# Scales by transposes and on-chip copies, K and V as single products between the transposes

## What is computed

```python
q = w8a8_linear(layernorm(x), wq, bq)          # rows and weights rounded to 127 levels
k, v = ctx @ wk.T + bk, ctx @ wv.T + bv        # fp32, 16 heads of 32
attn = softmax(q @ k.T / sqrt(32) + mask)
x = x + w8a8_linear(attn @ v, wo, bo)
h = gelu(int8_linear(layernorm(x), W1, B1))    # 512 -> 2048, scales per row
out = x + int8_linear(h, W2, B2)               # 2048 -> 512
```

## Time and profile before

| | |
|---|---|
| median of 3 runs | 748.97 us (744.27 to 751.18) |
| the profiled execution | 753.85 us, its span 751.9 us |
| granted TensorE clock, mean | 0.941 |
| instructions | 14564 |

### The profile page before, as it was taken

How to read it: one execution, slowest core, us unless ns; L and a number is a source line. 1 busy time by engine, 2 the same in 40 slices (tenths; PEclk the granted TensorE clock), 3 DMA queues, 4 the chain that set the end, 5 groups by cost and what they waited for, 6 DMA issues and landing times.

```text
span 751.9 us, 14564 instructions
## 1 busy us (share of the span) xinstructions
PE 633.2 (84%) x4936; PEld 474.4 (63%) x4986; DVE 469.8 (62%) x1101; ACT 444.6 (59%) x1085; POOL 300.4 (40%) x555
## 2 busy tenths in 40 slices
PE   1838779979797799989699899989897999998763
PEld 1736566857665576767668677867675686766421
DVE  6635667856774295667376665468554576856763
ACT  2316555757763384949369566668584587878400
POOL 4232433453544353545452444353461333231231
PEclk9988898998998899999899999999999999999967
DMA  9985297752324425451722525324323112201321
GB/s 290 254 87 129 69 173 182 231 90 67 59 51 79 45 40 100 34 95 39 68 72 38 99 17 111 52 49 39 98 52 67 35 36 54 55 24 13 64 49 42
DMA packets 92664, 61.07 MB, mean 81 GB/s; under 512 B 69952, under 2 KB 79936, under 8 KB 91952
## 3 DMA queue, kind: packets, MB, share of 16 engines
q1 hardware_dynamic: 92592, 60.15, 41.2%
HBM read 42.09 MB, written 3.69 MB: 61 GB/s over the span
## 4 chain that ended last, share of the span: by engine, by line
PE 43%; DMA 21%; DVE 11%; SPq 9%; issue 8%; POOL 5%; ACT 1%; DVEq 0%; POOLq 0%
PE ps_ring L869 10%; PE ps_t L889 7%; PE ps_ring L855 7%; DMA oqT<-o_q 5%; PE ps_ring L933 5%; DMA q_dram<-cols 4%; PE ps_s L880 4%; PE ps_ring L945 4%; PE ps_t L902 4%; SPq L344 3%; DMA hT<-h_q 3%; DMA yqT<-y_q 2%; DMA xT<-x_q 2%; DMA q_dram<-so_col 1%; DMA b_row<-in_w2T 1%
## 5 line engine op out<-in xcount | busy, mean ns | idle before, releaser
L577 ACT ACTIVATE probs<-probs,neg_max 112x375 f32<-112x375 f32 x256 | 153.6, 602 | 36.5 <-DVE neg_max L702 36.0
L587 ACT ACTIVATE pT<-ps_t 125x336 f32<-125x336 f32 x256 | 109.0, 446 | 93.3 <-PE ps_t L889 91.6
L702 DVE CUSTOM_DVE_ANT_0 probs<-ps_s,mask_in 112x375 f32<-112x375 f32 x256 | 127.0, 543 | 56.4 <-PE ps_s L880 49.0
L889 PE MATMUL ps_t<-ident,probs 112*125 112x112 f32 x768 | 149.5, 287 | 4.4 <-ACT probs L577 2.1
L889 PEld LDWEIGHTS ps_t<-ident,probs 112*125 112x125 f32 x768 | 125.3, 199 | 36.9 <-issue 17.2
L855 PE MATMUL ps_ring<-ctx_hi,wk_hi 128*128 128x376 f32 x256 | 95.6, 373 | 29.0 <-DVE wk_lo L608 15.8
L869 PE MATMUL ps_ring<-wv_hi,ctx_hi 128*125 128x512 f32 x192 | 86.3, 449 | 2.1 <-issue 2.0
L855 PE MATMUL ps_ring<-ctx_lo,wk_hi 128*128 128x376 f32 x256 | 87.8, 343 | 0.0
L855 PE MATMUL ps_ring<-ctx_hi,wk_lo 128*128 128x376 f32 x256 | 87.6, 342 | 0.0
L463 POOL TENSOR_TENSOR ctx_lo<-ctx_in,ctx_hi 128x376 fp32r<-128x376 f32 x64 | 66.7, 1068 | 49.7 <-ACT ctx_hi L557 48.8
L945 PE MATMUL ps_ring<-w_q,hT 128*128 128x512 bf16 x207 | 65.9, 417 | 19.0 <-DMA hT<-h_q 18.2
(11 more groups left out here) (107 smaller groups left out, 1071.4 us busy)
## 6 DMA issues: line engine op xcount, KB each, us to landing
ctx_in<-in_ctxT SPq DMA_DIRECT2D x32, 375.0 KB, 6.3
h<-in_w2T SPq DMA_DIRECT2D x4, 1024.0 KB, 9.0
b_row<-in_w2T SPq DMA_DIRECT2D x4, 1024.0 KB, 9.8
xres<-in_x SPq DMA_DIRECT2D x14, 256.0 KB, 2.8
x_in<-in_x SPq DMA_DIRECT2D x16, 224.0 KB, 4.3
out<-y SPq DMA_DIRECT2D x14, 256.0 KB, 2.7
mask_in<-in_mask SPq DMA_DIRECT2D x16, 164.1 KB, 3.9
w_q<-in_w1T SPq DMA_DIRECT2D x2, 1024.0 KB, 13.9
```

Source lines behind the costliest of these rows:

```text
L577: nc.scalar.activation(probs[:, hd % SP_RING, :], probs[:, hd % SP_RING, :], ACT.Exp, scale=-1.0, bias=neg_max[:, b % 2, hd:hd + 1], accum ...
L587: nc.scalar.activation(pT[0:LR, hd % PT_RING, :], att_bank("T", b, hd, 0)[0:LR, 0:LC * N], ACT.Copy).then_inc(pT_s, 1)
L702: nc.vector.tensor_tensor_reduce(out=probs[:, hd % SP_RING, :], in0=ps_s[hd % HG][0:N, 0:L], in1=mask_in[:, b % 2, :], scale=-1.0, scalar= ...
L889: last = nc.tensor.transpose(att_bank("T", b, hd, 0)[0:LR, lc * N:(lc + 1) * N], probs[:, hd % SP_RING, lc * LR:(lc + 1) * LR], ident[0:N, ...
```

## The change

x's scale: TensorE transposes the column, repeated over 128 columns, against the identity (`x`), which gives the repeated row in a `ps_t` bank; ScalarE copies it to `xs_bc`. `so` likewise (`O`), in a `ps_ring` bank. o's scale: one DMA from `o_s` to `os_col`, both in SBUF, per batch, two where the batch lies in two tiles (`p`, now `os_move`), with four columns instead of two. `s`, `l`, `e`, `f`, `i` are gone from the SP list. A letter `k` or `v` is now one product instead of three. All five lists are new. Counts of all other letters are the same.

```diff
-    "k": ("k", each(B, KC, KC)), "v": ("v", each(B, LC, KC)), "q": ("q", each(B)), "S": ("S", each(B, KC)),
+    "O": ("so", each()), "x": ("x_row", each(B)),
+    "k": ("k", each(B, KC, 3 * KC)), "v": ("v", each(B, LC, 3 * KC)), "q": ("q", each(B)), "S": ("S", each(B, KC)),
...
 PE_ORDER = (
-    "kkkkkkkkkkkkkkkkvvvvvvvvvvvvkkkkkkkkkkqkkkkkkvSvvvTTTvTTTTTTSTTTvMPvTTTTTTSTTTvTTTTTTPqTTTvTTTvTTTSvPvTTTTTTTTTk"
...
-    "TTTTSkdTdTdTdTdTdTddkPTkdTdTdTdTdTdkdTdTTTTTooookPkkkkkkkqSvvvvTTTTTTSuuuuuuTuTuTTTTuuuuTTTPuuuvvvTTTuvSTTTvvvvk"
...
-    "dTdTdTddPTdTdTTTTTTTPguuuuuuuuuuuuuuuuoooodddddddddddddddduuuuuuuuuuuuuuuudddddddddddddddd"
+    "xkkkvvvkkkvvkkkvvvkkkvvvvkkkkkkkkkkkkkkkkkkkkOkkkkvvvvvvvvvvvvvvvvvvvvvvvvkkkkkkqkkkkkkkkkkkkSkkkvvvvvvTTTTSTTTT"
...
+    "dSTkTkTkTkTTkqTkTkTkTkTTkkkTSoooovTvTvvvvvvvvvvvvPTvTvTvTvTvTvTvTvTvTvTvTvvvvvvuuuuvvvSvvPTuuuuuuuuTTuuuuTkTkTkk"
+    "kkkkkkSkTkTkTkTkTkTkkkkkkkkPTkTkTkTkTkTkkTkTkTkxSkkPgddddddddddddddddkTTkTkTkTTkkqTTkTkTkTTkkkTSoooovTvTvvvvvvvv"
...
+    "dddddPTTTddddooooddddTTTTTTTTTTTTTTTPPguuuuuuuuuuuuuuuuoooouuuuuuuuuuuuuuuudddddddddddddddddddddddddddddddd"
 )
 DVE_ORDER = (
...
-    "ySmSQqSSSSuSSSuSugSoSuSShhHymSQSSSudSSuSSquhSSSSuSSSSghoHSSSSySSSmQdguuouuhhHymQduuuuhhHd"
+    "SgodSSqSymQSSSSuSSuuSuShhSHSSgSoSSdSSymQSSSSSSuSuuuShghSHSSSoSSSSydmQgouuuuyhmhQHuuuuhhdHd"
 )
...
 POOL_ORDER = (
-    "nllllXrllllnqllllXnqllllXnqXllllnqbyrXllllHbynrqXHlllnlbyqrXnHllllXbynqrXnHllllbyqrXnHllllqXbynrHllllqXbynrHllll"
+    "nrXlllllllqnllXlllqnllllXnqXllqnllXbyqnrHlXlllnbyqrXHnlllqXlbyrHnllqXlbyrlHnllqXlbyrlHnllqXlbyrlHnllqXlbyrlHnllq"
...
 SP_ORDER = (
-    "rxmQCCWWWW1cmQWWWW1sCC1txXelCCft1slCCxXms2l2CpoCxX222s2lmxX2C2CpoisBlrYmxXCCpoiHrHYmslxXSHpHoiCrSsCYlxXmHsHpoCiC"
+    "WWWWcWxWWWrCCQm1Qm11xXCCtCt1CxXCCm222CC2po2xX2m22xXBCpoCmxXrYHpHoxXCSCmrYxXHHpoSCmxXrCYHHpoSCmxXrYCHHpoSCmxXrYCH"
...
+def parts(b):
+    cut = (b * N // P + 1) * P
+    return [(b * N, cut), (cut, (b + 1) * N)] if cut < (b + 1) * N else [(b * N, (b + 1) * N)]
...
+            def os_move(b):
+
                 sp.wait_ge(o_sc_s, b + 1)
-                sp.dma_start(os_dram[b * N:(b + 1) * N].unsqueeze(1), o_s[:]).then_inc(os_stored, 16)
-
-            def os_load(t):
-                sp.wait_ge(os_stored, 16 * batches_of(t))
-                wait_for(sp, y_mul, t - 1)
-                sp.dma_start(os_col[:, t % 2:t % 2 + 1], os_dram[t * P:(t + 1) * P].unsqueeze(1)).then_inc(os_in[t % 2], 16)
+                for row, end in parts(b):
+                    t = row // P
+                    wait_for(sp, y_mul, t - OS + 1)
+                    sp.dma_start(os_col[row % P:row % P + end - row, t % OS:t % OS + 1],
+                                 o_s[row - b * N:end - b * N, :]).then_inc(os_in, 16)
...
+            def x_row(b):
+                act.wait_ge(xrow_pe, b + 1)
+                wait_for(act, q_mul, b)
+                nc.scalar.activation(xs_bc[:], att_bank("x_row", b)[:, 0:N], ACT.Copy).then_inc(xs_s, 1)
...
+            def x_row(b):
+                pe.wait_ge(x_scaled, b + 1)
...
+                bank = att_free("x_row", b)
+                nc.tensor.transpose(bank[:, 0:N], x_s[:].broadcast_to([N, P]), ident[0:N, 0:N]).then_inc(xrow_pe, 1)
```

More of the change, by code:

```diff
@@ L37 @@
 ATT = 2
+OS = 4
 def each(*counts):
@@ L75 @@
     "1": ("w1_load", each(4)), "2": ("w2_load", each(8)), "B": ("b1_load", each()),
-    "e": ("so_store", each()), "f": ("so_load", each()),
-    "X": ("x_T", each(B)), "s": ("xs_store", each(B)), "l": ("xs_load", each(B)),
-    "o": ("o_T", each(B)), "p": ("os_store", each(B)), "i": ("os_load", each(TILES)),
+    "X": ("x_T", each(B)), "o": ("o_T", each(B)), "p": ("os_move", each(B)),
     "Y": ("y_T", each(TILES)), "H": ("h_T", each(TILES, 2)),
@@ L850, in k_unit @@
                 bank = bank_of("k", b, g, 0)
[L851 to L857 removed]
+                if part == 0:
+                    if b == 0:
+                        pe.wait_ge(w_lo_s, k + 1)
+                    pe.wait_ge(ctx_lo_s, KC * b + k + 1)
@@ L858, in k_unit, with v_unit @@
+                w_half, x_part = ((wk_hi, ctx_hi), (wk_hi, ctx_lo), (wk_lo, ctx_hi))[part]
+                last = nc.tensor.matmul(bank[:, 0:LP], w_half[:, k, cols], x_part[:, p, k, :],
+                                        start=(step == 0), stop=(step == 3 * KC - 1))
+                if step == 3 * KC - 1:
                     last.then_inc(k_pe, 1)
-            def v_unit(b, lc, k):
-                p, rows = b % 2, slice(lc * LR, (lc + 1) * LR)
-                if k == 0:
+            def v_unit(b, lc, step):
+                p, rows, k, part = b % 2, slice(lc * LR, (lc + 1) * LR), step // 3, step % 3
+                if step == 0:
@@ L863, in v_unit @@
                     ring_bank("v", b, lc, 0)
                 bank = bank_of("v", b, lc, 0)
-                if b == 0:
-                    pe.wait_ge(w_lo_s, KC + k + 1)
-                pe.wait_ge(ctx_lo_s, KC * b + k + 1)
-                for t, (x_part, w_half) in enumerate(((ctx_hi, wv_hi), (ctx_hi, wv_lo), (ctx_lo, wv_hi))):
-                    last = nc.tensor.matmul(bank[0:LR, :], x_part[:, p, k, rows], w_half[:, k, :],
-                                            start=(k == 0 and t == 0), stop=(k == KC - 1 and t == 2))
@@ L871, in v_unit @@
-                if k == KC - 1:
+                if part == 0:
+                    if b == 0:
+                        pe.wait_ge(w_lo_s, KC + k + 1)
+                    pe.wait_ge(ctx_lo_s, KC * b + k + 1)
+                x_part, w_half = ((ctx_hi, wv_hi), (ctx_hi, wv_lo), (ctx_lo, wv_hi))[part]
+                last = nc.tensor.matmul(bank[0:LR, :], x_part[:, p, k, rows], w_half[:, k, :],
+                                        start=(step == 0), stop=(step == 3 * KC - 1))
+                if step == 3 * KC - 1:
```

154 lines of the change are left out of this document (74 added, 80 removed).

## The result

The changed kernel takes 675.68 us (median of 4, 674.34 to 676.3), the kernel before 750.08 beside it (744.27 to 752.14): ratio 0.902, 95% interval 0.896 to 0.907. A few executions of a kernel come out slower for no reason of the kernel's own; they are left out of the medians and ranges in this text.

A forecast was written before the change was run, and what follows sets the result against it. TensorE's own work was taken to bound the middle, latency chains both ends. Terms of -20, -14, +7, -3, -11, +5, -4 sum to -40 us: 753.85 to 714 profiled, median 709, own range 698 to 722, wider range 682 to 742.

The forecast's parts named there:

- first rival: Idle time of the middle closes almost wholly, as the new pattern covers each chain: median 672 us; chance 0.17.
- What bounds the kernel: TensorE's own work bounds the middle, latency chains both ends; o's transpose (6.2 us) completes just after the store (7.3).
- Output scales, -20: On-chip copies land in 2.5 us instead of 7.3, nearly ending TensorE's wait before output projection: -20 us (-5 to -28.6).
- The other chains and the clock, -14: Waits before `up` and `down` and low clock behind idle stretches shrink in the new order: -14 us (0 to -40).
- K and V mixed, +7: Single products between transposes: 451 more lone transposes cost 4.5 us, 17 new ones 3: +7 us (+3 to +12).
- x's scales, -3: 32 transfers leave SP's queue for TensorE transposes and ScalarE copies; fewer table loads, cover not path: -3 us (0 to -10).
- The start, -11: K starts near 23 us, q near 40, scores near 45, first gather at 80 instead of 96: -11 us (0 to -20).
- The new slack, +5: Scores may wait for VectorE's mask, standing 1.3 us behind the transpose that frees the buffer: +5 us (0 to +36).
- rival "slower": Turn of transpose, mask and scores costs 2.5 us at each of 36 close places: 794 us; chance 0.12.
- The end, -4: Chains of y and o shorten at the end, against two absmax in y's chain (2.4 us): -4 us (0 to -8).
- The floor, 671: TensorE's busy 633 us plus the idle start and end (23 + 15) cannot go: 671 us.
- The signs it named: If right: oqT lands in 2.4-3 us, copies <3, oqT wait <8, first-last gather <590, scores <50, K >20.

The follow-up runs named there:

- path_only: The changed kernel's scale path (transposes on TensorE, on-chip copies) with the old order of the work; 679.64 us, ratio 0.917 to the kernel before.
- before_all_spread: Kernel before, only addresses changed: output scales 1,792 bytes apart in memory, x's scales 8 bytes apart; 674.68 us, ratio 0.912.
- dummy_store: Changed kernel plus one unread store per batch of 112 scales to neighbouring memory addresses, ahead of o's transposing DMA; 747.2 us.
- dummy_behind: Changed kernel plus one unread store per batch of 112 scales to neighbouring memory addresses, behind o's transposing DMA; 716.75 us.
- triples: Changed kernel with the three probability transposes of a head issued together where the first stood; 678.02 us.
- xs_memory: Changed kernel with x's scales alone stored to memory and loaded back, output scales still copied on chip; 745.16 us.
- start_tail: Changed kernel with start reordered (x's and context's loads first) and tile 13's norm no longer split by two row maxima; 667.77 us.
- before_spread: Kernel before with output scales stored 1,792 bytes apart in memory, x's scales as they were; 694.65 us, ratio 0.937.

## Why the prediction was wrong

Its first rival (the idle time closes almost wholly, 672 us) came true in its number, at a chance of 0.17, but not for its reason: it had the new pattern cover each chain, and path_only and before_all_spread reach 680 and 675 us with the old one. By its own steps:

**What bounds the kernel.** Right in kind. The link that it drew, "the transpose completes just after the store ahead of it", is shown by dummy_store. That only the transpose was held is the step that failed: the 6.3 us landing of the context's load stood on the same page of the profile, and in dummy_behind the context's load (6.8 us), x's load (7.9) and y's rows (8.8) behind the store are late as well. Nor was it memory as a target that made the store slow, as the prediction read the 7.3 us: to far addresses in memory it lands in 1.7, as the copies on chip do.

**Output scales, -20.** The copy landed in 1.7 us (taken: 2.5), the wait went wholly. In the middle it had been 26.4 us of the 34.9. The size of the wait was read rightly. The pattern with 16 d, 12 k, 13 T, a q and an S before `oooo` stands seven times in the list, not nine (and once with a second S), which changes nothing here. The remedy was not the copy on chip as such but any destination that isn't near.

**The other chains and the clock, -14.** The term most mis-sized. Of the middle's 53 us, 46 are idle time, 26 of them oqT's; so 20 are other waits (yqT 9.5, xT 5.2, hT some 5), and the clock rose from 0.96 to 1.00, at most 22 us more (half of 44). That makes 68; TensorE's other busy time must then have risen by some 15 in this stretch, of which the next term and the shifted K and V work (6) are a part. So this term gave up to 42 us (20 + 22), or 27 after all that grew (53 - 26), where the forecast took 14 within bounds of 0 and -40. The low clock was in the bound and hardly in the choice, although it follows the same waits that the first term had just removed. That these waits and the slow stretches came from the near stores, and not from an order that covered its chains unevenly, is shown by before_all_spread: the old order, middle 521 us, clock 1.00.

**K and V mixed, +7.** A lone transpose behaves as foreseen; TensorE in order of time:

```profile
156.90 0.26 PE L910 MATMUL ps_t<-ident,probs 112*125 112x112 f32 x1
156.93 0.42 PE L875 MATMUL ps_ring<-ctx_hi,wk_lo 128*128 128x376 f32 x1
157.19 0.26 PE L910 MATMUL ps_t<-ident,probs 112*125 112x112 f32 x1
```

0.29 per pair, so 0.12 for the transpose. The 4.5 us for 451 more of them don't show against triples (612.2 and 612.0 us busy). Of the +7, the rest was for new transposes, which are 20 and not 17, as `O` is four.

**x's scales, -3.** The table loads fell to 26 as counted. But x's stores were costed as cover, and xs_memory puts stores and loads together at 69 us in the new order. The trace of before had two signs of it: xT's landing of 3.9 us, which nothing explained, and a second wait of SP besides the 52.7 us that the prediction read, before the load of x's row:

```profile
SPq L390 <- DMA q_dram<-cols: 37.2, 6, 9.2
```

**The start, -11.** It gave 20, the bound: K began at 25.7 us (said: 23), q at 45 (40), first scores at 49 (45), gather at 76 (80), and the clock's records show no fall up to there, where 0.91 had meant 17 us at 1.2 GHz. The new order isn't needed for it: path_only, whose K starts at 16.5 us as before, has its first gather at 77.

**The new slack, +5.** Nothing. VectorE waits for TensorE's transposes 30.0 us in 43 pieces, and no wait of TensorE's scores for a mask is among TensorE's waits. The rival "slower" did not come.

**The end, -4.** Nothing, 45.3 against 45 us. Two row maxima of 1.21 us lie in y's chain, as said, and the yqT of tile 12 came so late that its up products ran at 631.4 to 636.5, ahead of the last projection, which had been ready since 634. start_tail gets 4 us back.

**The floor, 671.** Its reasoning was wrong: it took TensorE's busy 633 us as fixed, while part of it was work at 1.2 GHz. With the middle at 2.4 GHz the same work takes 612. The changed kernel stayed 5 us above 671 all the same, and start_tail came 3 below it.

**The signs it named.** Those of the right side all came (oqT 2.4, copies 1.7, wait for oqT 0, first to last gather 552 under 590, first scores 49, K past 20). They could not tell 709 from 676, since they were set at the size of the forecast.

## What to carry to other kernels

When a store of many 4-byte elements to memory must be, place them 16 bytes or more apart, or keep them on the chip; the gain was the same in the old order (675 and 680 us). Before a reordering is costed, look whether transfers that have nothing to do with a chain also land late, for then one cause holds them all. In these traces the time at 1.2 GHz came with waits, so removing a wait gave back its length and about half of the slow stretch that followed. A count of busy time is a floor only after it is taken at full clock.

## What was not expected of the hardware

- 112 writes of 4 bytes to neighbouring places in memory land in 6 to 10 us (median 7.3), and other transfers behind them land 3 to 7 us later than without them (medians of dummy_behind against the changed kernel); 16 bytes apart they land in 1.7 and oqT behind them in 2.4, as without a store. Neighbours in one row of SBUF land in 1.9.
- The eight stretches at 1.2 GHz in the middle of the kernel before, 44 us together, each began in a wait of TensorE of 2.7 to 6.2 us or right behind it; the changed kernel's middle has no such wait and no such stretch, with 768 transposes in both.
- A strided load of 128 such elements from memory landed in 1.9 us (before_spread), against 3.0 from neighbours in the kernel before, where near stores of the output scales were also under way; the two are not separated.
